# Row numbers ahead of their scatters, first expert rows ahead of the query tables, first transposition behind the last query group

## The reference

```python
xn = _layernorm(x, axis=-1)
x = x + _L0_attn_ref(xn, ...) + _L0_ffn_ref(xn, L0_ffn_router_w, L0_ffn_w1, L0_ffn_w2)
...
# _L0_ffn_ref
logits = jnp.einsum('btd,ed->bte', x, router_w)
top_vals, top_idx = jax.lax.top_k(logits, K)              # K = 2 of E = 8
top_w = jax.nn.softmax(top_vals, axis=-1)
h = jnp.square(jax.nn.relu(jnp.einsum('nd,edh->enh', xf, w1)))   # H = 512
y = jnp.einsum('enh,ehd->end', h, w2)
out = w_f-weighted sum of y[idx_f, n]                      # the two chosen experts
```

## Time and profile before

| | |
|---|---|
| median of 3 runs | 758.07 us (757.8 to 762.49) |
| the profiled execution | 760.31 us, its span 758.6 us |
| TensorE busy | 705.8 us, 93% of the span |
| VectorE, ScalarE, GpSimd busy | 560.0, 453.2, 454.6 us |
| mean granted TensorE clock | 0.981 |

### The profile page before, as it was taken

One profiled execution on the slowest core, in us unless ns is written; L12 is line 12 of the kernel. 1 busy time (PEld: TensorE's weight loads), 2 busy tenths in 40 slices (PEclk: granted clock), 3 DMA queues, 4 the chain that ended last, 5 costly groups with the idle time before them and its releaser, 6 DMA issues.

```text
span 758.6 us, 19586 instructions
## 1 busy us (share of the span) xinstructions
PE 705.8 (93%) x6224; PEld 631.0 (83%) x6224; DVE 560.0 (74%) x1295; ACT 453.2 (60%) x959; POOL 454.6 (60%) x577
## 2 busy tenths in 40 slices
PE   6999995799999999999998999899999899999994
PEld 4999842799999999999977999777778678888883
DVE  4999771587878888788658886599898777676732
ACT  5666482576776677755525888456677664544411
POOL 3677776799788797988422223034376555655363
PEclk9999997999999999999999999799999999999998
DMA  8699573344445344444178985145457755666352
GB/s 240 183 265 328 185 170 99 90 126 115 129 135 143 104 121 140 130 122 115 41 207 264 313 278 172 30 96 123 109 111 187 223 203 134 148 149 149 50 57 28
DMA packets 151106, 113.99 MB, mean 150 GB/s; under 512 B 59359, under 2 KB 141282, under 8 KB 151012
## 3 DMA queue, kind: packets, MB, share of 16 engines
q1 hardware_dynamic: 137812, 86.94, 41.2%
q0 software_dynamic: 12624, 25.35, 13.4%
q10 hardware_dynamic: 576, 0.53, 0.3%
HBM read 68.68 MB, written 40.80 MB: 144 GB/s over the span
## 4 chain that ended last, share of the span: by engine, by line
PE 85%; DVE 6%; issue 3%; ACT 2%; DMA 1%; POOL 1%; SPq 0%; POOLq 0%; ACTq 0%; DVEq 0%
PE banks L939 13%; PE bank L1195 11%; PE bank L904 11%; PE banks L1206 5%; PE bank L995 5%; PE banks L834 4%; PE bank L915 4%; PE bank L1102 3%; PE banks L770 3%; PE bank L1085 3%; PE banks L823 3%; PE banks L1012 3%; PE bank L776 3%; PE bank L1074 2%; PE bank L887 2%
## 5 line engine op out<-in xcount | busy, mean ns | idle before, releaser
L939 PE MATMUL banks<-r_split,rt_split 128*128 x852 | 110.6, 284 | 1.0 <-issue 0.9
L2297 POOL DMA_INDIRECT ults_by_choice_and_token<-rw,y_id x71 | 79.2, 1115 | 46.5 <-ACT rw L1403 36.3
L939 PEld LDWEIGHTS banks<-r_split,rt_split 128*128 128x128 f32 x852 | 104.9, 191 | 1.6 <-issue 1.6
L904 PE MATMUL bank<-wqkv_split,rt_split 128*128 128x256 f32 x560 | 88.5, 290 | 3.9 <-DVE rt_split L1818 3.8
L1195 PE MATMUL bank<-r_split 128*128 128x512 f32 x384 | 89.6, 391 | 1.3 <-issue 1.1
L1195 PEld LDWEIGHTS bank<-r_split 128*128 128x128 f32 x384 | 71.4, 188 | 16.3 <-issue 1.9
L904 PEld LDWEIGHTS bank<-wqkv_split,rt_split 128*128 128x128 f32 x560 | 77.6, 193 | 5.9 <-DVE rt_split L1818 5.7
L2396 POOL DMA_INDIRECT out_x<-r,idx x32 | 50.2, 1569 | 52.9 <-DVE r L2155 45.2
L2266 POOL DMA_INDIRECT rows_by_expert<-rw,slots x64 | 67.2, 1051 | 18.6 <-issue 9.8
L1818 DVE TENSOR_TENSOR rt_split<-r,rt_split 128x512 fp32r<-128x512 f32 x56 | 59.8, 1108 | 20.0 <-ACT rt_split L1326 20.0
L1843 DVE TENSOR_TENSOR rt_split<-rw,rt_split 128x512 fp32r<-128x512 f32 x71 | 62.9, 918 | 7.4 <-ACT rt_split L1396 7.1
(11 more groups left out here) (284 smaller groups left out, 1768.2 us busy)
## 6 DMA issues: line engine op xcount, KB each, us to landing
rt<-in_w SPq DMA_DIRECT2D x24, 512.0 KB, 4.7
rw<-rows_by_expert SPq DMA_DIRECT2D x71, 128.0 KB
r<-in_w SPq DMA_DIRECT2D x16, 512.0 KB
rt<-ults_by_choice_and_token SPq DMA_DIRECT2D x32, 256.0 KB, 3.9
rw<-in_x SPq DMA_DIRECT2D x16, 256.0 KB, 4.7
rw<-in_sin_q SPq DMA_DIRECT2D x32, 128.0 KB
rw<-x_layer SPq DMA_DIRECT2D x16, 256.0 KB
x_plus_bias<-rw SPq DMA_DIRECT2D x16, 256.0 KB, 3.2
```

What stands on the lines that cost most here:

```text
L904: last = pe.matmul(bank[1 + b][:, k * 2 * P:(k + 1) * 2 * P], w[:, c, o:o + P], x[d % 2][:, c, :], start=n == 0, stop=n == 3 * DC - 1)
L939: last = pe.matmul(bank[6 + t % 2][:, 0:D], hidden_T(h, t, c), w[:, ds(e2, 1), o + c * D:o + (c + 1) * D], start=n == 0, stop=n == 3 * HC - 1)
L2297: pool.indirect_dma_start(y0_d[:, :], bass.IndirectOffsetOnAxis(y_id[:, t:t + 1].bitcast(I32), 0), c_y[:, t % XB, :], None, bounds_check=l ...
```

## The change

Three edits. On SP the loads of the first four row tiles come ahead of the query tables 2 to 5. On TensorE the first transposition comes behind the last query group, and on ACT its high part behind the copy of that group, while the first expert weights' high part stays ahead of it. On POOL the numberings are taken out of `scatter_x`: one large `iota` of 16 words per partition numbers the first 8 pairs for choice 0 before the first slots are there, and that of choice 1 of pair h = g-1 now stands between the two scatters of choice 0 of pair g, with the wait for the landed scatters ahead of it and the wait for its own end behind the second of these scatters.

```diff
             sp.wait_ge(zero_out, 16 * (E + 1))
+            for t in range(XB):
+                load_rows(t)
             for i in range(2, 4):
                 load_tables(i)
                 load_xq(i)
-            for t in range(XB):
-                load_rows(t)
             for i in range(4, QE):
                 load_tables(i)
...
             for g in range(3, NQ):
-                if g == NQ - 1:
-                    transpose_rows(0)
                 project(g)
                 if g - 3 in range(NB):
                     weigh_values(g - 3)
+            transpose_rows(0)
...
                 if g == NQ - 1:
-                    high_rows_T(0)
                     high_w1(0)
                 copy_q(g)
...
+            high_rows_T(0)
...
-            def scatter_x(g, k):
-                if k == 0:
+            def number_rows(g, k, n=1):
+
+                ins = pool.iota(a_xn[:, g % NX:g % NX + n, :, D:D + 1].bitcast(I32), pattern=[[GT * P, n], [P, GT], [0, 1]],
+                                base=GT * g * P + k * N, channel_multiplier=1)
+                chain[0] += 1
+                ins.then_inc(pseq, 1)
+                return chain[0]
+
+            def scatter_x(g, k, j):
+                pool.indirect_dma_start(xs0_d[:, :], bass.IndirectOffsetOnAxis(slots0_v[:, k, GT * g + j:GT * g + j + 1], 0),
+                                        a_xn[:, g % NX, j, :], None,
+                                        bounds_check=last_slot, oob_is_err=False).then_inc(sc0_out[g % 4], 16)
+
+            first_ids = number_rows(0, 0, NX)
+            for g in range(NG + 1):
+                if g < NG:
+                    if g >= NX:
+                        pool.wait_ge(sc0_out[g % 4], 16 * TOPK * GT * ((g - NX) // 4 + 1))
+                        first_ids = number_rows(g, 0)
                     pool.wait_ge(slot_r, g + 1)
                     if g >= 4:
                         pool.wait_ge(sc0_out[g % 4], 16 * TOPK * GT * (g // 4))
-                else:
-                    pool.wait_ge(sc0_out[g % 4], 16 * TOPK * GT * (g // 4) + 16 * GT)
-                link(pool.iota(a_xn[:, g % NX, :, D:D + 1].bitcast(I32), pattern=[[P, GT], [0, 1]],
-                               base=GT * g * P + k * N, channel_multiplier=1))
-                for j in range(GT):
-                    pool.indirect_dma_start(xs0_d[:, :], bass.IndirectOffsetOnAxis(slots0_v[:, k, GT * g + j:GT * g + j + 1], 0),
-                                            a_xn[:, g % NX, j, :], None,
-                                            bounds_check=last_slot, oob_is_err=False).then_inc(sc0_out[g % 4], 16)
-
-            for g in range(NG + 1):
+                    pool.wait_ge(pseq, first_ids)
+                    scatter_x(g, 0, 0)
+                if g >= 1:
+                    h = g - 1
+                    pool.wait_ge(sc0_out[h % 4], 16 * TOPK * GT * (h // 4) + 16 * GT)
+                    second_ids = number_rows(h, 1)
                 if g < NG:
-                    scatter_x(g, 0)
+                    scatter_x(g, 0, 1)
                 if g >= 1:
-                    scatter_x(g - 1, 1)
+                    pool.wait_ge(pseq, second_ids)
+                    for j in range(GT):
+                        scatter_x(h, 1, j)
```

## The result

| | before | changed |
|---|---|---|
| median of 11 runs | 758.29 us (757.64 to 762.49) | 766.37 us (761.12 to 771.28) |
| ratio | | 1.009, 95% interval 1.0059 to 1.012 |
| profiled execution | 760.31 us, span 758.6 | 761.12 us, span 759.4 |
| last scatter starts | 116.04 | 119.90 |
| first row load by SP | 123.76 | 123.40 |

The changed kernel is 0.9% slower. The medians are 8.1 us apart, but the ratio, which is taken over all fast executions of both kernels, gives 6.8 us, and the text goes by it. The profiled execution is the fastest of its eleven; where it was lucky stands further down.

The account below looks back on a forecast made before the run. TensorE carries 85% of the chain but waits at 118 to 128 us for the end of POOL's scatters. Scatters +4.5, the rest -1.6, sum +2.9 us: 761.0 against the median of 758.07; range 758 to 764, 8-in-10 range 754 to 766.

Parts of the forecast that it names:

- The moved wait: On POOL, room for landings ahead of second numberings falls from 6.4 to 5.0 us: five waits, +7.0 us; other bound +1.4.
- The end of the scatters: POOL's chain of 64 scatters ends 4.5 us later, range +0.5 to +7, and releases the expert stage.
- The numberings: On POOL, eight of 32 numberings leave the scatter chain for one large one: 0.9 us saved at the most.
- the other 16: POOL numberings now between two scatters of another group without their own wait: gain between 0 and 1.8 us, taken as 0.
- SP's order: On SP, first row load leaves 4.5 us earlier, but row tiles 4 and 5 queue behind tables, so transposition 2 gains nothing.
- TensorE's order: Last query group runs before the first transposition; first hidden pair 8 us earlier, second 1.8; gain 1.6 us (0.6 to 2.6).
- from 142 us on TensorE is bound as before and hands the difference through: On TensorE after the second hidden pair, the summed +2.9 us was to pass unchanged to the kernel's end.
- the cover of 1 us ahead of transposition 3: Row tiles 6 and 7 land near 147.2, transposition 3 due near 148; cover was 3.8 us; if gone, gain shrinks towards 0.6.
- A: Rival: landings come at fixed instants, scatters end 0.5 to 2 us late, the rest gives 1.6 back: 757 to 758.5; chance 0.26.
- B: Rival: numberings hide, landings shorten to under 5 us, scatters end 1 to 2.7 us earlier: middle 754.5; chance 0.16.
- C: Rival: POOL's lag makes ACT's normalisation wait 3 us for second scatters; scatters 9 to 11 us late, 766 to 768; chance 0.10.
- D: Rival: the first hidden pair's 8 us come through, SP's tables 4 and 5 not delaying row tiles 4 and 5: 750; chance 0.05.

Follow-up runs that it names:

- the B batches: Timing batches B1 and B2 of the follow-up kernels, each against its own executions of the kernel before, which takes 787.1 us in B1 and 786.97 us in B2.
- batch A: Timing batch of four follow-up kernels, each against its own executions of the kernel before, which takes 759.78 us there (23 executions).

## Why the prediction was right, and where not

The forecast was 761.0 with a range of 754 to 766 and "within 1%" as the likeliest class. The measured ratio puts the changed kernel 6.8 us above before (4.5 to 9.1), which is 764.9 on the 758.07 that the forecast started from: inside the range and the class, though the interval reaches a little over 1%. The median itself, 766.37, is 0.4 above the range. The direction and the mechanisms were right, the size was not: +2.9 was forecast. Of the 3.9 us between, POOL's half took 0.9 (5.4 measured, 4.5 forecast) and the half of SP and TensorE 2.1 (+0.5 measured, -1.6 forecast); 0.9 is what the halves leave of the whole, which the noise covers.

**The moved wait: right.** The steps (a landing takes 7.2 us in the full stretch, the numbering had 6.4 and now has 5.0) appear one by one: the landing of 36.85 took 7.1 us, there are nine waits in place of five, 8.0 us in place of 4.0. The kernel with this move alone undone is at 1.0033, the whole at 1.009. The end of the scatters was forecast at +4.5 (0.5 to 7); the profiles have +3.9 and, for POOL's edit alone, +5.9, the ratio of that edit 5.4 us. Waits for landings grew by 4.1 us in this trace and 5.3 in that one, between the two bounds that I gave for them (1.4 and 7.0). The waits added up, but not to the full 7.0 that I had argued for. The Trainium skill ("DMA: Bandwidth & Descriptors", section on queues, rings and completion order) says that each DMA engine goes round between the queues that have work, packet by packet. The landing of 7.1 us in the stretch that is full of other transfers agrees with it, but no run here tells it from other reasons.

**The numberings: a right sum from two wrong terms, which is luck.** From the first to the last scatter POOL takes 95.4 us before and 99.95 after, +4.5. From the two lists of waits: landings +4.1; idle with nothing shown +3.3 (9.8 to 13.1); idle behind a numbering about -0.8; slots +0.4; the numberings themselves -1.1 (31 to 24 of 0.15 us); the scatters' own time -1.1 (67.2 to 66.1); together +4.8. I had -0.9 for everything about the numberings, where these rows give +1.4 (3.3 - 0.8 - 1.1), and 5.4 for the landings, where they have 4.1. That the sum was the +4.5 of the forecast owes to these two errors, of opposite sign. The step that failed is "8 are still directly ahead of their scatter (groups 8 to 15, choice 0), and gain nothing". They lose: with the waits for slots, for older scatters and for their own end packed between numbering and scatter, POOL stands 0.81 us and not 0.28, eight times, 4.2 us. For the other 16 I took the bound 0, and the truth was the other one: the numbering between two scatters of another pair is covered, 36.85 is 1.32 us after the scatter of 35.53, and its neighbours without a numbering are 1.28 to 1.31 us apart. But mending the packed waits alone did not bring 4 us back, because the landings took them.

**SP's order: right.** First row load 3.5 us behind the start of the last scatter where it was 7.7 before, rotation 2 after its tables, tables 4 and 5 behind it, row tiles 4 and 5 behind these, transposition 2 waiting: expected at 119.3, 128.5, 133.0, 134.9 and 138.9, found at 123.40, 132.66, 137.52, 139.29 and 143.35, all 4.1 to 4.5 us later, of which the lag of the scatters is 3.9. The row of POOL for rotation 2:

```profile
132.66 0.46 POOL L2297 TENSOR_TENSOR rw<-r,rw 128x128 f32<-128x128 f32 x1 [6.62 <-DMA rw<-in_sin_q]
```

**TensorE's order: the term that was mis-sized.** Forecast -1.6 us (0.6 to 2.6 of gain), measured +0.5 (-0.8 to +1.9), so that even the smallest gain of the range is only just within the interval. The mechanism up to the second hidden pair is as described: it starts 2.4 us later than before while the scatters end 3.9 later, a gain of 1.5. After that it melts: measured against the scatters' end the gain is 1.2 at the first `result0` (148.88 against 146.18), 0.7 at transposition 3 (153.04 against 149.91), and 0.2 at the last transposition (377.7 against 374.0). The step that failed is "from 142 us on TensorE is bound as before and hands the difference through". I had named the weak place, the cover of 1 us ahead of transposition 3, as the thing that shrinks the gain towards 0.6; it shrank to nothing, through 0.27 us of wait there, a hidden pair of 4.95 us in place of 4.64, and waits later in the stage that I did not take apart. In the kernel with these edits alone the wait ahead of transposition 3 is 0.95 us.

**The rivals.** A (landings at fixed instants) is refuted as a forecast of the time, 757 to 758.5, in the first comparison. Part of its mechanism showed in the kernel with the packed waits mended: what POOL saves it stands still at the next landing. B fell: landings did not shorten (median 6.1 us, 36 to 80 us, against 6.2). C gave 766 to 768, which is nearest to the measured median, but its mechanism was only touched: ACT waited once, 1.1 us where C has 3, for second scatters, the last normalisation starts at 78.3 against 77.6, and the scatters end 3.9 us late and not 9 to 11. D fell at the place named. None of these covers the B batches, where another stretch holds the kernel up.

**The profiled execution.** Its 761.12 us would have made the change look like +0.8 us. The last transposition is 3.7 us later than before, yet the end only 0.8. The difference lies in a later stage. Here are its first four transposing matmuls, before and changed:

```profile
484.27 1.12 PE L1074 MATMUL bank<-ident,rw 128*128 128x128 f32 x4 [0.42 <-ACT rw L1510]
...
487.42 0.66 PE L1073 MATMUL bank<-ident,rw 128*128 128x128 f32 x4 [0.45 <-ACT rw L1509]
```

The granted clock in 480 to 500 us was 1.00 in this execution. Busy time by stretch, us, busy us by engine, clock, DMA share, GB/s, of the changed kernel:

```profile
480.00:500.00 20.00, 15.40 (x288) 12.45 (x287) 15.77 (x54) 9.96 (x20) 0.84 (x3) 1.00 0.23 41
```

and of POOL's edit alone in batch A, whose end keeps the lag:

```profile
480.00:500.00 20.00, 16.27 (x240) 14.40 (x238) 11.19 (x41) 9.59 (x20) 0.60 (x2) 0.77 0.14 28
```

The kernel before had 0.74 there, and the other three traces of batch A 0.66 to 0.74, so only this profile has the high level throughout. The first of these groups (line 1073, before 1074) is at 487.4 against 484.3, the last at 598.9 against 598.1: the lag of 3.1 us has fallen to 0.8 between them. That the clock alone did this is the likely reading, but no run changes the clock by itself. The other ten executions had a mean clock of 0.974 to 0.979, this one 0.984.

## What to carry to other kernels

A wait that is moved ahead of other work must be costed with the landing times of the stretch it sits in, not of the whole trace: 1.4 us less room for each turned five short waits into nine. When an instruction loses its own wait, look at what other waits now stand between it and its reader. A head start in one place is worth only what the next transfer behind it in the same queue allows. And undo each half alone, in more than one batch if it can be had: here the halves were worth +5.4 and +0.5 us where the kernel before takes 760 us, and -3.3 and +2.8 where it takes 787.

## What the runs showed of the hardware

- Three semaphore waits between a 0.15 us numbering and the scatter that reads it cost 0.81 us, one costs 0.28, and with the two other waits put ahead of the numbering it was at most 0.3 again. A numbering between two scatters that do not need it cost almost nothing, 1.32 us from scatter to scatter against 1.28 to 1.31 beside it.
- The same program took 759.8 us in one batch of runs and 787 us in two others. In a trace from the slow batches matmuls of the front end are spaced by up to 1.0 us and ACT stands 3.2 to 6.6 us at a time. Not explained.
- The granted clock of one stage, 480 to 500 us, was 1.00 in one execution and 0.66 to 0.77 in five others, of other kernels of this set; the stage's first four transposing matmuls took 0.66 us in the first and 1.12 in the kernel before. The lag that went away between 487 and 599 us was 2.3 us, as much as some of the changes studied here.
